# A bias seeded into PSUM by ScalarE, and every second one-hot matrix made by GpSimd

## The reference, cut to what matters

```python
ei = jnp.concatenate([x[src], edge_attr], axis=-1)          # 50000 x 320
core = jnp.maximum(ei @ W1 + b1, 0.0) @ W2 + b2
gate = jax.nn.sigmoid(ei @ Wg + bg)
msg = gate * core
agg = jax.ops.segment_sum(msg, dst, num_segments=x.shape[0])
out = agg + x
...                                                          # layer norm of out
```

## Time and profile before

| What | us |
|---|---|
| median of three runs (lowest, highest) | 1700.47 (1699.43, 1701.69) |
| span of the profiled execution | 1691.9 |
| median less span | 8.6 |
| TensorE busy in the span | 1511.9 (89%) |
| VectorE busy | 1469.6 (87%) |
| ScalarE busy | 1202.7 (71%) |
| GpSimd busy | 1036.2 (61%) |

### The profile page before, as it was taken

One profiled execution on the slowest core, in us unless ns is written; L12 is line 12 of the kernel. 1 busy time (PEld: TensorE's weight loads), 2 busy tenths in 40 slices (PEclk: granted clock), 3 DMA queues, 4 the chain that ended last, 5 costly groups with the idle time before them and its releaser, 6 DMA issues. The chain is left out here.

```text
span 1691.9 us, 40433 instructions
## 1 busy us (share of the span) xinstructions
PE 1511.9 (89%) x10735; PEld 1378.6 (81%) x10735; DVE 1469.6 (87%) x3257; ACT 1202.7 (71%) x2896; POOL 1036.2 (61%) x1093
## 2 busy tenths in 40 slices
PE   6879999999999999999669688999998999999874
PEld 3669999999999999999459567787787887777653
DVE  4559999999999999999577689999999999999866
ACT  1458888888888888888056367777776767777573
POOL 0446666666666666664176577777777777777316
PEclk9989999999999999999979899999999999999888
DMA  4356666666666666665125787777777777777813
GB/s 135 138 184 186 187 186 186 186 187 186 187 187 188 185 188 185 187 184 145 33 82 191 221 245 220 231 228 231 227 228 224 225 229 227 229 226 223 281 46 97
DMA packets 164893, 318.92 MB, mean 188 GB/s; under 512 B 30231, under 2 KB 103928, under 8 KB 164436
## 3 DMA queue, kind: packets, MB, share of 16 engines
q0 software_dynamic: 66560, 219.06, 44.8%
q1 hardware_dynamic: 98132, 97.49, 18.7%
HBM read 291.90 MB, written 24.53 MB: 187 GB/s over the span
## 5 line engine op out<-in xcount | busy, mean ns | idle before, releaser
L493 POOL DMA_INDIRECT gath<-edge_in_tab,idx x392 | 413.6, 1055 | 270.5 <-DVE gate_in L933 207.6
L1226 PE MATMUL bank<-weighted,hot 128*128 128x260 f32 x880 | 238.6, 395 | 30.7 <-ACT hot L749 29.6
L506 POOL DMA_INDIRECT kept_more<-kv_tab,idx x176 | 195.5, 1111 | 60.6 <-issue 39.3
L1226 PE MATMUL bank<-w_lo,relu_hi 128*128 128x256 f32 x784 | 221.8, 283 | 0.0
L1226 PE MATMUL bank<-w_hi,relu_lo 128*128 128x256 f32 x784 | 221.7, 283 | 0.0
L1226 PE MATMUL bank<-w_hi,relu_hi 128*128 128x256 f32 x784 | 221.1, 282 | 0.0
L1226 PEld LDWEIGHTS bank<-weighted,hot 128*128 128x128 f32 x880 | 153.2, 192 | 53.4 <-ACT hot L749 36.7
L644 ACT ACTIVATE relu_hi<-bank 128x512 fp32r<-128x512 f32 x196 | 117.4, 599 | 81.4 <-PE bank L1226 81.4
L506 POOL DMA_INDIRECT hs<-kv_tab,idx x132 | 148.1, 1122 | 41.3 <-issue 36.3
L506 POOL DMA_INDIRECT xs<-kv_tab,idx x132 | 141.0, 1068 | 48.7 <-issue 22.7
L1229 PE MATMUL bank<-ident,gath 128*128 128x128 f32 x784 | 150.1, 273 | 10.6 <-DMA gath<-edge_in_tab,idx 10.6
(11 more groups left out here) (284 smaller groups left out, 4924.4 us busy)
## 6 DMA issues: line engine op xcount, KB each, us to landing
block_row<-row_tab SPq DMA_DIRECT2D x440, 64.0 KB
ea_in<-in_ea SPq DMA_DIRECT2D x392, 64.0 KB, 2.4
edge_in_tab<-node_row SPq DMA_DIRECT2D x26, 256.0 KB, 2.0
kv_tab<-qkv_row SPq DMA_DIRECT2D x25, 258.0 KB, 2.5
gath<-edge_in_tab,idx POOLq DMA_INDIRECT x392
xs<-in_x SPq DMA_DIRECT2D x1, 3328.0 KB, 15.2
v_in<-kv_tab SPq DMA_DIRECT2D x25, 130.0 KB, 2.1
rows_tab<-hs SPq DMA_DIRECT2D x25, 128.0 KB, 2.4
```

What stands on the lines that cost most here:

```text
L493: g.indirect_dma_start(gath[:, q, i, :], None, edge_in_tab, bass.IndirectOffsetOnAxis(ap=idx[:, half, q, i:i + 1], axis=0)).then_inc(gath_ ...
L506: g.indirect_dma_start(kept(u, 0, KVW)[:, i, :], None, kv_tab, bass.IndirectOffsetOnAxis(ap=idx1[:, half, u % BATCH, i:i + 1], axis=0)).th ...
L1226: return nc.tensor.matmul(out_, lhsT=lhs, rhs=rhs, start=start, stop=stop)
```

## The change

1. b2 is loaded twice into `b2_rows`, 128 rows in full f32, in place of `b2_sb`; `b2_parts` with its cast and its subtraction is gone. In the chunk loop ScalarE has a new stage `seed`, lag 2, between `one_hot` and `distances`: it copies `b2_rows` (128x512) into bank 4 or 5, once per chunk. `core` waits for it and adds its twelve products onto what stands in the bank (start=False), without the two products of `share` and `b2_parts`.
2. ScalarE makes `dist` and `hot` for even blocks only, `dist` with one buffer. For odd blocks GpSimd writes the one-hot matrix by two compares (`is_equal`, 128x128 each), in a stage `odd_one_hot` of lag 5. Late blocks stay with VectorE.
3. GpSimd's gathers are written out as straight code with the indices read from `src_chunk` directly; `idx`, its copy and a semaphore increment per chunk are gone.
4. Seven semaphores of the head are merged into two (`lists_made`, `tallies_made`), with the same waits in the same places.

```diff
@@ -359,7 +357,8 @@
                 sp.dma_start(w_edge[rows, 0:HID], w1[HID:HID + EDGE_DIM, :]).then_inc(w_in, 16)
                 sp.dma_start(w_edge[rows, HID:], wg[HID:HID + EDGE_DIM, :]).then_inc(w_in, 16)
             sp.dma_start(w2_sb[:], w2.rearrange("(c p) n -> p c n", p=P)).then_inc(w_in, 16)
-            sp.dma_start(b2_sb[:], b2.to_broadcast([2 * SHARES, HID])).then_inc(w_in, 16)
+            for i in range(2):
+                sp.dma_start(b2_rows[:, i, :], b2.to_broadcast([P, HID])).then_inc(w_in, 16)
             for i in range(2):
                 sp.dma_start(ln0_sb[:, i, :], ln0[i:i + 1, :].to_broadcast([P, HID])).then_inc(lw_in, 16)
             sp.dma_start(query_sb[:], query_col).then_inc(lw_in, 16)
...
@@ -479,19 +478,18 @@
             g.affine_select(out=upto[:], in_=upto[:], compare_op=ALU.is_ge, fill=0.0, base=0,
                             pattern=[[1, HALF_C]], channel_multiplier=-1).then_inc(consts, 1)
-            def gather_node_rows(first, u, half, turn=0):
-                b, q = first + u, u % SLOTS
-                if q == 0:
-                    g.tensor_copy(idx[:, half, :, :], src_chunk[:, ds(b, SLOTS), :]).then_inc(idx_done, 1)
-                after(pool, gate_added, b - SLOTS + 1)
-                if q == 0:
-                    pool.wait_ge(idx_done, turn + 1)
-                pool.sem_inc(idx_seen, 1)
+            def gather_node_rows(c):
+                after(pool, gate_added, c - SLOTS + 1)
                 for i in range(2):
-                    g.indirect_dma_start(gath[:, q, i, :], None, edge_in_tab,
-                                         bass.IndirectOffsetOnAxis(ap=idx[:, half, q, i:i + 1], axis=0)).then_inc(gath_in[q], 16)
+                    g.indirect_dma_start(gath[:, c % SLOTS, i, :], None, edge_in_tab,
+                                         bass.IndirectOffsetOnAxis(ap=src_chunk[:, c, i:i + 1], axis=0)).then_inc(gath_in[c % SLOTS], 16)
+            def odd_one_hot(b):
+                if b % 2 == 1:
+                    after(pool, sum_ready, b - 1)
+                    for i in range(2):
+                        last = g.tensor_scalar(hot[:, 1, i, :], iota_node[:], rel_col[:, b, i:i + 1], None, ALU.is_equal)
+                    last.then_inc(pool_hot_done, 1)
             def gather_keys_values(first, u, turn=0):
                 b, half = first + u, u // BATCH
...
@@ -516,11 +514,7 @@
                 g.tensor_tensor(xs[:, w, :], xs[:, w, :], ln0_sb[:, 1, :], ALU.add).then_inc(beta_added, 1)
             for q in range(2):
                 pool.wait_ge(row_stored[q], 16 * (WPAD // 2))
-            for u in range(SLOTS):
-                gather_node_rows(0, u, 0)
-            with pool.Fori(0, (CHUNKS - SLOTS) // (2 * SLOTS)) as k:
-                for u in range(2 * SLOTS):
-                    gather_node_rows(2 * SLOTS * k + SLOTS, u, 1 - u // SLOTS, 2 * k + 1 + u // SLOTS)
+            chunks_and_blocks(pool, [(gather_node_rows, 0, CHUNKS), (odd_one_hot, 5, CHUNKS)])
             pool.wait_ge(sum_added, BLOCKS)
...
@@ -601,11 +595,10 @@
             s = nc.scalar
             act.wait_ge(consts, 1)
             s.mul(share[:], ones_c[0:2 * SHARES, 0:P], 1 / SHARES).then_inc(act_consts, 1)
-            act.wait_ge(w_in, 9 * 16)
+            act.wait_ge(w_in, 10 * 16)
             s.copy(w_node_hi[:], w_node[:]).then_inc(w_hi_done, 1)
             s.copy(w_edge_hi[:], w_edge[:]).then_inc(w_hi_done, 1)
             s.copy(w2_hi[:], w2_sb[:]).then_inc(w_hi_done, 1)
-            s.copy(b2_parts[:], b2_sb[:]).then_inc(w_hi_done, 1)
             def normed(done):
                 def stage(k, q):
...
@@ -656,17 +649,26 @@
             def distances(b):
-                after(act, hot_done, b - 1)
-                for i in range(2):
-                    last = s.activation(dist[:, b % 2, i, :], iota_node[:], ACT.Square, bias=rel_col[:, ds(b, 1), i], scale=-1.0)
-                last.then_inc(dist_done, 1)
+                if b % 2 == 0:
+                    after(act, hot_done, b // 2)
+                    for i in range(2):
+                        last = s.activation(dist[:, i, :], iota_node[:], ACT.Square, bias=rel_col[:, ds(b, 1), i], scale=-1.0)
+                    last.then_inc(dist_done, 1)
             def one_hot(b):
-                act.wait_ge(dist_done, b + 1)
-                after(act, sum_ready, b - 1)
-                s.activation(hot[:, b % 2, :, :], dist[:, b % 2, :, :], ACT.Relu, bias=one_col[:], scale=-1.0).then_inc(hot_done, 1)
-            chunks_and_blocks(act, [(split_edges, 0, CHUNKS), (one_hot, 4, CHUNKS), (distances, 3, CHUNKS), (relu_inner, 2, CHUNKS),
+                if b % 2 == 0:
+                    act.wait_ge(dist_done, b // 2 + 1)
+                    after(act, sum_ready, b - 1)
+                    s.activation(hot[:, 0, :, :], dist[:], ACT.Relu, bias=one_col[:], scale=-1.0).then_inc(hot_done, 1)
+            def seed(n):
+                if n < 2:
+                    act.wait_ge(row_ready, WPAD)
+                after(act, msg_done, n - 1)
+                s.copy(bank[4 + n % 2][:], b2_rows[:].rearrange("p i f -> p (i f)")).then_inc(seeded, 1)
+            chunks_and_blocks(act, [(split_edges, 0, CHUNKS), (one_hot, 4, CHUNKS), (seed, 2, CHUNKS), (distances, 3, CHUNKS), (relu_inner, 2, CHUNKS),
                                     (high_message, 4, CHUNKS), (gates, 3, CHUNKS)])
...
@@ -1324,16 +1325,21 @@
                     last = mm(to, ea_parts[:, slot, i * P:(i + 1) * P], w_edge_lo[:, HID:], False, True)
                 last.then_inc(gate_ready, 1)
+            def onto(out_, lhs, rhs):
+                return nc.tensor.matmul(out_, lhsT=lhs, rhs=rhs, start=False, stop=False, skip_group_check=True)
             def core(n):
+                pe.wait_ge(seeded, n + 1)
                 pe.wait_ge(relu_lo_done, n + 1)
                 for i in range(2):
                     to = bank[4 + n % 2][:, i * HID:(i + 1) * HID]
-                    mm(to, share[:], b2_parts[:], True, False)
                     for c in range(2):
                         tile = slice(c * CHUNK + i * P, c * CHUNK + (i + 1) * P)
-                        mm(to, relu_hi[:, n % 2, tile], w2_hi[:, c, :], False, False)
-                        mm(to, relu_hi[:, n % 2, tile], w2_lo[:, c, :], False, False)
-                        last = mm(to, relu_lo[:, n % 2, tile], w2_hi[:, c, :], False, c == 1)
+                        onto(to, relu_hi[:, n % 2, tile], w2_hi[:, c, :])
+                        onto(to, relu_hi[:, n % 2, tile], w2_lo[:, c, :])
+                        last = onto(to, relu_lo[:, n % 2, tile], w2_hi[:, c, :])
                 last.then_inc(core_ready, 1)
             def sum_messages(b):
...
@@ -1347,7 +1353,10 @@
                     last.then_inc(sum_ready, 1)
                     return
                 pe.wait_ge(msg_lo_done, b + 1)
-                pe.wait_ge(hot_done, b + 1)
+                if b % 2 == 0:
+                    pe.wait_ge(hot_done, b // 2 + 1)
+                else:
+                    pe.wait_ge(pool_hot_done, b // 2 + 1)
                 to = bank[6 + b % 2][:, 0:HID]
                 for i in range(2):
                     mm(to, hot[:, b % 2, i, :], msg_hi[:, b % 2, i, :], i == 0, False)
```

More of the change, by code:

```diff
@@ L93, in build @@
         rel0_row = sb(ctx, "rel0_row", [HEADS, BATCHES], f32)
-        idx = sb(ctx, "idx", [P, 2, SLOTS, 2], i32)
         ht_hi = sb(ctx, "ht_hi", [P, 2, 2, P], f32r)
@@ L108, in build @@
             w2_lo = sb(l0, "w2_lo", [P, 2, HID], f32r)
-            b2_parts = sb(l0, "b2_parts", [2 * SHARES, HID], f32r)
+            b2_rows = sb(l0, "b2_rows", [P, 2, HID], f32)
             ea_in = sb(l0, "ea_in", [P, SLOTS, CHUNK], f32)
@@ L117, in build @@
             msg_lo = sb(l0, "msg_lo", [P, 2, 2, HID], f32r)
-            dist = sb(l0, "dist", [P, 2, 2, P], f32)
+            dist = sb(l0, "dist", [P, 2, P], f32)
             hot = sb(l0, "hot", [P, 2, 2, P], f32r)
@@ L240, in build @@
         d_step = sem("d_step")
-        counted, cumulated, sel_ready, rows_ready, off_ready, cols_ready, meta_ready = (
-            sem(n) for n in ("counted", "cumulated", "sel_ready", "rows_ready", "off_ready", "cols_ready", "meta_ready"))
+        lists_made, tallies_made, meta_ready = sem("lists_made"), sem("tallies_made"), sem("meta_ready")
         w_hi_done, w_lo_done, wqkv_hi_done, wqkv_lo_done, bo_hi_done, bo_lo_done = (
@@ L249, in build @@
         gath_in, ea_arrived = sems("gath_in", SLOTS), sems("ea_arrived", SLOTS)
-        idx_done, ea_hi_done, ea_lo_done, z_ready, relu_hi_done, relu_lo_done, gate_done, core_ready = (
-            sem(n) for n in ("idx_done", "ea_hi_done", "ea_lo_done", "z_ready", "relu_hi_done", "relu_lo_done",
+        ea_hi_done, ea_lo_done, z_ready, relu_hi_done, relu_lo_done, gate_done, core_ready = (
+            sem(n) for n in ("ea_hi_done", "ea_lo_done", "z_ready", "relu_hi_done", "relu_lo_done",
                              "gate_done", "core_ready"))
@@ L256, in build @@
```

(29 more changed lines are left out.)

6 lines of the change are left out of this document (2 added, 4 removed).

## The result

The changed kernel took 1798.82 us (median of four runs, 1798.2 to 1802.34), before 1699.95 us (four runs): ratio 1.0608, 95% interval 1.0585 to 1.063. It is slower by 98.9 us; 1798 was forecast.

A forecast was written before the change was run, and what follows sets the result against it. TensorE was taken to bound the chunk loop at 3.53 us; two new loops through several engines would make it 4.05 a chunk, 195 x 4.05 = 789.8 against 692.1, 97.7 us more: 1798 us, range 1728 to 1850.

The forecast's parts named there:

- TensorE's 3.53 us a chunk: First layer's chunk loop before the change: 30 matmuls without a gap set the pace, 3.53 us a chunk.
- VectorE's 3.32: VectorE's own floor in the chunk loop, 3.32 us; as the pace it would save 45 us, the most to gain.
- The first loop: VectorE's msg, ScalarE's seed to msg_hi, back to VectorE: 3.76 us for even n, 4.24 for odd, mean 4.00.
- The second loop: VectorE's gate_in, GpSimd's gathers and compares, TensorE's products, back to msg: 8.18 us for two chunks, 4.09 a chunk.
- VectorE's stalls: Fetch stalls before hs, 12.8 us in all, may come onto the path: 0 to 10 us, taken as 0.05 a chunk.
- 8.6 us "around the span": Time of the median 1700.47 us outside the profiled span of 1691.9, claimed to stay the same.
- Straight gathers: GpSimd's program written out removes an idx copy in four chunks and the loop's branch, off the path: 0.
- Merged semaphores: Changed semaphore names in the head were claimed to cost nothing: the same waits in the same places.
- Rival 3: GpSimd's compares block VectorE's msg_lo at a shared SBUF port: 4.51 us a chunk, 1888 us; chance 0.05.
- the low end of 0.292: Lower bound for one GpSimd 128x128 compare, from a one-input operation; GpSimd's loop would be 7.84 us, 3.92 a chunk.

The follow-up runs named there:

- e6: Changed kernel with the two bias products kept and no seed, odd blocks' compares one pair of gathers earlier (lag 4): 1694.11 us, 0.999 of the kernel before.
- e3: Changed kernel with seed moved behind gates on ScalarE and GpSimd's compares at lag 4 instead of 5: 1662.94 us, 0.9819 of the kernel before.
- e7: Changed kernel with seed behind gates and every one-hot matrix on ScalarE, no compares on GpSimd: 1660.7 us, 0.9783 of the kernel before.
- e2: Changed kernel with GpSimd's compares one pair of gathers earlier (lag 4 instead of 5), seed left in place: 1782.16 us, 1.0521 of the kernel before.
- e1: Changed kernel with seed moved behind gates, to the end of ScalarE's step, compares left at lag 5: 1778.46 us, 1.0507 of the kernel before.
- e4: Kernel before with GpSimd's gathers written out as straight code and nothing else changed: 1695.36 us, 1.0006 of the kernel before.
- r1: The changed kernel itself, measured again beside the other candidates on one chip: 1799.15 us, 1.0606 of the kernel before.

## Why the prediction was right

**The bound.** TensorE's 3.53 us a chunk with VectorE's 3.32 behind it: e6 is back at the first, e3 and e7 run at 3.39, which I read as VectorE's 3.32 and its stalls. TensorE's 28 products, 3.30, lie so close that no run tells the two apart.

**The first loop.** Forecast 4.24 and 3.76, measured alone in e2 4.24 and 3.66. The unmeasured price, ScalarE's copy into PSUM, was taken at 0.52 from start to start and measured 0.53 (501.33 to 501.86). The 0.10 too much is nearly all `relu_hi` up to `msg_hi` in the even step, for which I took 0.58; it was 0.49 (506.10 to 506.59), about the same as with much work queued. VectorE's 0.84 from `msg_lo` to `hs` after a wait, and the hand-overs 0.04 and 0.14, came out within a hundredth.

**The second loop.** Forecast 8.18, measured 8.16, but its terms were not as good as its sum:

| Link, us | forecast | measured |
|---|---|---|
| `msg` to end of `gate_in` | 1.87 | 1.88 |
| up to the first gather | 0.81 | 0.28 |
| gather, pause, gather | 2.44 | 2.42 |
| two compares | 0.92 | 1.24 |
| hand-over to TensorE | 0.05 | 0.15 |
| sum, core, hand-over | 2.09 | 2.19 |

The start of the gather was read from the hardware loop and is 0.53 shorter in straight code; I had named that possibility and kept the long value. The compare is 0.60, not 0.46. The rest is 0.10 of hand-over to TensorE and 0.10 in the products, most of it behind the first, whose successor starts 0.19 later (506.58 to 506.77) and not 0.12. The errors cancel, and that is luck. With only the gather's start right the loop is 7.65, ScalarE's 8.00 decides and the forecast stays; with only the compares right it is 8.50, 4.25 a chunk, and I would have said 1837 us.

**Which loop decides.** I took 4.05 between two loops and added 0.05 for VectorE's stalls to ScalarE's. GpSimd's decides, by some 0.25 us in two chunks, and e1 and e2 show how little that says: neither repair alone gave back more than 17 us. My own sum for that loop, 4.09, would have given 105 us more. The pace with stalls is 4.085, 0.035 more than forecast, 7 us over 195 steps: the loop became 104.4 us longer, not 97.7. That the first medians lie only 98.9 apart is not the loop's doing. At TensorE's pace it takes the same time whatever the execution, from first to last `msg` 692.1 us in before, 691.7 in e4 and 691.8 in e6, in spans of 1691.9, 1687.3 and 1693.0; what varies lies outside it. In r1 the medians are 103.8 us apart (1799.15 and 1695.39). So that 97.7 is close to 98.9 is luck too, and the forecast was some 6 us short. The 8.6 us "around the span" were not a fixed cost either: every run of the experiments took 1.7 to 1.9 us longer than its own span, so the profiled execution of before was a short one.

**The small terms.** Straight gathers 0: 1.0006. Merged semaphores were not tried alone; with the loop accounting for 104.4 of the 105.2 us between the first two profiles, there is little room for them or for the second load of b2. Rival 3, the shared port, I had looked for between the compares and `msg_lo` and given 0.05. No `msg_lo` of the changed kernel is lengthened (0.681 to 0.694 us); what there is of it is the longer gather, 0.16 us in two chunks, if the port is its cause.

## What to carry to other kernels

Before work is moved to an engine with idle time, look at what it waits for and what is queued behind it there: here the copy itself was free. Its wait, a few instructions too early in ScalarE's list, made a loop through two engines that alone costs 88 us against before (e2), and the compares, one pair of gathers too late in GpSimd's, made another that alone costs 86 (e1). Walk each new wait round until it comes back to the same instruction one or two turns later, and add the starts up; the longest such loop is the pace. If two loops are near each other, repair both before you judge either.

## What the runs showed of the hardware

Gathers that start while VectorE runs `msg_lo`, which has both inputs in SBUF, took longer here, by somewhat less than what was left of `msg_lo`. In e3:

```profile
501.54 0.69 DVE L953 TENSOR_TENSOR msg_lo<-msg,msg_hi 128x512 fp32r<-128x512 f32 x1
```

```profile
501.63 1.51 POOL L484 DMA_INDIRECT gath<-edge_in_tab,src_chunk  x1 [0.17 <-issue]
503.44 0.95 POOL L484 DMA_INDIRECT gath<-edge_in_tab,src_chunk  x1 [0.30 <-issue]
```

At 501.63 0.60 us of `msg_lo` are left, and the gather takes 1.51 in place of 0.95. With 0.38 left it is 1.19, with nothing such under way 0.95; with 0.29 left 1.11 (504.08 in the changed kernel). Over the gathers that start from 200 to 600 us it is the same: before, the 110 that start within `msg_lo` take 1.10 to 1.20, mean 1.17, those that start beside `msg`, `relu_lo` or `hs`, each with one operand in PSUM, 0.94 to 0.97. In the changed kernel no `msg_lo` is slowed in return; in e3 a few are, the most this one, which starts 0.50 us before the second of two compares ends (768.65 + 1.18) and takes 0.81 in place of 0.69:

```profile
769.33 0.81 DVE L953 TENSOR_TENSOR msg_lo<-msg,msg_hi 128x512 fp32r<-128x512 f32 x1
```

```profile
768.65 1.18 POOL L491 TENSOR_SCALAR hot<-iota_node,rel_col 128x128 fp32r<-128x128 f32 x2 [2.77 <-PE bank L1227]
```

The Trainium skill (SBUF — State Buffer, "SBUF: two separate sides") has such a VectorE instruction exclude a GpSimd one that reads SBUF. The longer gathers agree with that in size, 0.56 us more with 0.60 left; the `msg_lo` above was held up by 0.12 us and not by the 0.50 that were left. That a gather is such an instruction was only seen side by side, not tried by itself.

A GpSimd compare of 128x128 takes some 0.60 us, two 1.21, where scaling the 219 elements at 0.797 by size gave 0.47: the time doesn't shrink in proportion to the row. The Trainium skill (GPSIMD Engine Reference, Engine selection) has one-input work at about line rate, which I had set beside the low end of 0.292; the trace is at twice that, so it doesn't bear this out at this size. And a gather in straight code follows the `gate_in` that releases it after 0.27 us (e4), in the hardware loop with its register work after 0.81.
